# Sorting a step earlier in two equal parts, with the row transfers of a mixture-of-experts stage spaced by heads and tiles

## What is computed

```
# att1: 16 heads, q from x, k and v from the context
h = relu(out @ W1 + b1)
x = x + (h @ W2 + b2)
# moe1
xf = layernorm(x)                              # 2048 tokens of 128
routing = softmax(xf @ router_w.T)             # 8 experts
top_w, top_i = top_k(routing, 2); top_w /= sum(top_w)
h = silu(xf @ w_gate[e].T) * (xf @ w_up[e].T)  # 256 wide
x = x + sum over the two chosen e of top_w[e] * (h @ w_down[e].T)
```

## Time and profile before

| | us |
|---|---|
| median of 3 runs | 875.87 |
| lowest, highest | 874.03, 876.32 |
| profiled execution, its own time | 878.39 |
| its span, first to last instruction | 876.5 |

### The profile page before, as it was taken

How to read it: one execution, slowest core, us unless ns; L and a number is a source line. 1 busy time by engine, 2 the same in 40 slices (tenths; PEclk the granted TensorE clock), 3 DMA queues, 4 the chain that set the end, 5 groups by cost and what they waited for, 6 DMA issues and landing times. The chain is left out here.

```text
span 876.5 us, 14671 instructions
## 1 busy us (share of the span) xinstructions
PE 720.8 (82%) x4784; PEld 488.2 (56%) x4784; DVE 483.1 (55%) x1392; ACT 394.7 (45%) x837; POOL 238.3 (27%) x382
## 2 busy tenths in 40 slices
PE   1587888899988667978958787799999786779998
PEld 1355666566655435645525454567777675546665
DVE  4468676777777503623656874673335334444443
ACT  2465555466665525533424465353334554222221
POOL 4345454344321261224456643100001002000000
PEclk9999999999999977998967999799999999579999
DMA  9533224222230011222273320000000200023332
GB/s 294 140 96 86 64 65 117 70 69 68 76 85 16 11 46 46 88 82 82 70 193 87 90 75 2 1 1 1 1 0 1 82 0 1 1 79 104 97 94 63
DMA packets 76319, 57.94 MB, mean 66 GB/s; under 512 B 7400, under 2 KB 70120, under 8 KB 75768
## 3 DMA queue, kind: packets, MB, share of 16 engines
q1 hardware_dynamic: 74200, 52.85, 21.3%
q0 software_dynamic: 2048, 4.20, 1.5%
HBM read 25.37 MB, written 9.24 MB: 39 GB/s over the span
## 5 line engine op out<-in xcount | busy, mean ns | idle before, releaser
L909 DVE TENSOR_REDUCE negmax<-ps 128x2 f32<-128x512 f32 x256 | 169.8, 686 | 105.7 <-PE ps L1950 104.0
L1645 ACT ACTIVATE exps<-ps 128x512 f32<-128x512 f32 x256 | 148.3, 598 | 103.0 <-PE ps L1962 92.1
L1950 PE MATMUL ps<-stack 96*128 96x256 bf16 x512 | 102.6, 294 | 33.3 <-DVE negmax L909 19.3
L1962 PE MATMUL ps<-stack 99*128 99x256 bf16 x512 | 100.1, 286 | 22.6 <-DMA stack<-maxt 13.2
L1950 PEld LDWEIGHTS ps<-stack 96*128 96x128 bf16 x512 | 47.8, 103 | 58.2 <-DVE negmax L909 34.1
L1962 PEld LDWEIGHTS ps<-stack 99*128 99x128 bf16 x512 | 43.9, 101 | 63.8 <-DMA stack<-maxt 22.4
L1978 PE MATMUL ps<-exps,values 128*32 128x256 f32 x1024 | 72.9, 402 | 0.7 <-ACT exps L1645 0.7
L2203 PEld LDWEIGHTS ps<-pack_moe,ht 128*128 128x128 f32 x512 | 61.9, 191 | 15.8 <-issue 14.0
L1286 DVE SCALAR_TENSOR_TENSOR x_sb<-ps,weights,x_sb 128x128 f32<-128x128 f32 (+1 forms) x128 | 36.0, 344 | 61.7 <-PE ps L2203 61.6
L1819 ACT ACTIVATE ht<-ps,pack_moe 128x512 f32<-128x512 f32 x64 | 43.3, 686 | 57.5 <-PE ps L2291 56.0
L2203 PE MATMUL ps<-pack_moe,ht 128*128 128x128 f32 x512 | 62.3, 275 | 0.5 <-ACT ht L1819 0.5
(11 more groups left out here) (221 smaller groups left out, 1330.4 us busy)
## 6 DMA issues: line engine op xcount, KB each, us to landing
stack<-qk_parts SPq DMA_DIRECT2D x168, 128.0 KB
stack<-weights_t SPq DMA_DIRECT2D x32, 256.0 KB, 3.3
pack_moe<-in_moe SPq DMA_DIRECT2D x1, 3076.0 KB, 14.9
outputs_moe<-y_kept SPq DMA_DIRECT2D x46, 64.0 KB
ht<-gathered SPq DMA_DIRECT2D x22, 128.0 KB
gathered<-y_kept SPq DMA_DIRECT2D x10, 256.0 KB, 2.9
pack_moe<-in_moe SPq DMA_DIRECT2D x1, 2129.0 KB
pack_moe<-in_moe SPq DMA_DIRECT2D x1, 1732.0 KB, 6.9
```

The costliest lines, as they stand in the source:

```text
L909: dve.tensor_reduce(negmax_of[b % 2][:, :, h:h + 1].rearrange("p t h -> p (t h)"), ps[:, h % 2, :].rearrange("p (t k) -> p t k", t=2), AX, ...
L1645: nc.scalar.activation(exps[:, i, :], ps[:, 2 + h % 2, :], ACT.Exp, scale=scale)\
L1950: last = pe.matmul(ps[:, h % 2, t * T:(t + 1) * T], st[0:MAXROW, h, 0, t * P:(t + 1) * P], st[0:MAXROW, h, 1, :], start=True, stop=True)
L1962: last = pe.matmul(ps[:, 2 + h % 2, t * T:(t + 1) * T], st[0:MAXROW + 3, h, 1, t * P:(t + 1) * P], st[0:MAXROW + 3, h, 0, :], start=True, ...
```

## The change

The parts become equal: FIRST_PART = 4, 8 and 8 token tiles, 23 and 23 sorted tiles. Since the first part now needs only batches 0 to 3, its sorting stands a step earlier (the logits at (-1, 15), the two picks, the marks, the ranks and the places in step 0, the weights at (1, 12)), and the batches 4 to 6 are normalized at the end of the flow, with two more chunks turned in step 2. Of the tile loop's own sorting only the last two token tiles are normalized and turned there, and its steps come up to two tiles earlier.

The row transfers of the first part, now 16, are issued one every second beat from (0, 14), each with a wait on `cols_psum`, PE's count of the heads that have passed L1962. In the second part, also 16 now, and in the first 16 fetches, only every fourth waits for a tile (from tile 5 and from tile 25).

The offsets are read with three registers at (2, 6), and then with one load of one register behind the up product of each tile. Two waits are added in `turn_max` on PE, since a PSUM bank is shared otherwise.

The core of the diff:

```
@@ -80,11 +80,10 @@
...
 EXPERT = {"moe1": 768}
 PARTS = 2
-FIRST_PART = 5
+FIRST_PART = 4
 PART = (range(0, 2 * FIRST_PART), range(2 * FIRST_PART, NT))
-NORMED = (range(0, 8), range(8, 10), range(10, NT))
-CHUNKS = ((0, 1, 2, 3), (4, 5, 6, 7), (8, 9), (10, 11, 12, 13), (14, 15))
-FIRST_CHUNK = 3
+NORMED = (range(0, 8), range(8, 14), range(14, NT))
+CHUNKS = ((0, 1, 2, 3), (4, 5, 6, 7), (8, 9, 10, 11), (12, 13), (14, 15))
...
@@ -100,21 +99,23 @@
...
-SORT_STEPS = {"stats": ((-1, 6), (0, 3)), "rstd": ((-1, 7), (0, 4)), "norm": ((-1, 9), (0, 7)), "logits": (0, 12),
-              "top": (1, 1), "exp": (1, 1), "first": (1, 2), "second": (1, 3), "mark": (1, 3), "rank": (1, 7),
-              "place": (1, 4), "weigh": (1, 5), "load": (2, 6)}
-TURN_STEPS = ((-1, 11), (-1, 13), (0, 10))
-SEND_STEPS = ((1, 4, range(0, 5)), (2, 4, range(5, 10)))
+SORT_STEPS = {"stats": ((-1, 3), (2, 3)), "rstd": ((-1, 4), (2, 4)), "norm": ((-1, 8), (2, 6)), "logits": (-1, 15),
+              "top": (0, 1), "exp": (0, 2), "first": (0, 4), "second": (0, 6), "mark": (0, 8), "rank": (0, 9),
+              "place": (0, 11), "weigh": (1, 12), "load": (2, 6)}
+TURN_STEPS = ((-1, 10), (-1, 12), (2, 13), (2, 15))
+TURNED_STEPS = ((-1, 11), (-1, 13), (3, 0), (3, 1))
+SEND_FROM = 14
 ZERO_STEPS = range(-14, -2)
 ZEROINGS = len(ZERO_STEPS) + 1
-SORT_BEATS = {"norm": (-1, 0), "turn": (0, 1), "logits": 2, "top": 3, "exp": 3, "first": (4, 5), "second": (6, 7),
-              "mark": 7, "rank": 7, "place": (8, 9, 11), "weigh": 10}
-EARLY_TILES = (34, 35, 37, 38, 40, 41, 43, 45)
-JOIN_TILES = (32, 33, 35, 36, 38, 40, 42, 43)
+SORT_BEATS = {"turn": -1, "logits": 0, "top": 1, "exp": 1, "first": (2, 3), "second": (4, 4), "mark": 5, "rank": 5,
+              "place": (6, 7, 9), "weigh": 8}
+EARLY_TILES = (33, 34, 36, 37, 39, 41, 43, 45)
+JOIN_TILES = (30, 31, 33, 34, 35, 37, 39, 40)
 FETCHED_EARLY = 4
 IN_FLIGHT = 3
-SEND_TILE = 13
-FETCH_TILE = 27
+REGISTERS = 3
+SEND_TILE = 5
+FETCH_TILE = 25
...
@@ -523,7 +524,7 @@
...
             if s in SORTED:
-                return (TURN, TURN, TURN, 5, 6)[i]
+                return (TURN, TURN, 0, 1, 5)[i]
             return (0, 1, 0, 6)[i] if s in MOE else (6, SIDE, 6, 6)[i]
...
@@ -1198,14 +1200,12 @@
...
                 at = SORT_BEATS
-                if j in at["norm"]:
-                    apply_all(s, len(NORMED) - 1, CHUNKS[FIRST_CHUNK + at["norm"].index(j)])
                 if j == at["top"]:
                     route_logits(s, 1)
                 if j in at["first"]:
                     route_pick(s, 1, (0,), at["first"].index(j))
-                if j in at["second"]:
-                    route_pick(s, 1, (1,), at["second"].index(j))
+                if j == at["second"][0]:
+                    route_pick(s, 1, (1,))
                 if j == at["mark"]:
                     mark_picks(s, 1)
...
@@ -1469,9 +1470,9 @@
...
                             if (tail, u) == SORT_STEPS["rstd"][i]:
                                 make_rstd_all(nxt, i, NORMED[i])
-                        for at_tail, at_beat, tiles in SEND_STEPS if nxt in SORTED else ():
-                            if (tail, u) == (at_tail, at_beat):
-                                send_rows(nxt, 0, tiles)
+                        n, odd = divmod(16 * tail + u - SEND_FROM, 2)
+                        if nxt in SORTED and not odd and 0 <= n < 2 * len(GROUPS[nxt][0]):
+                            send_row(nxt, 0, n // 2, n % 2)
                         b = total + tail + 3
                         if flow == EARLY[0] and u in (3, 7) and valid(b) and b >= FETCHED_EARLY:
...
@@ -1496,20 +1497,22 @@
...
                         pool.tensor_tensor(kact, krelu, krelu, ALU.mult).then_inc(sem["kact_ready"], 1)
...
-            def send_rows(s, g, tiles):
-
-                if tiles[0] == GROUPS[s][g][0]:
+            def send_row(s, g, t, k):
+
+                n = 2 * (t - GROUPS[s][g][0]) + k
+                i, landed = sending(s, t, k)
+                if n == 0:
                     pool.wait_ge(zeros_out, 16 * ZEROINGS) if s == SORTED[0] and g == 0 else None
                     wait(pool, "placed_ready", s, 0, g)
-                for t in tiles:
-                    for k in range(2):
-                        i, landed = sending(s, t, k)
-                        if landed > 16:
-                            pool.wait_ge(sent[i], landed - 16)
-                        if g == 1:
-                            wait(pool, "taken_psum", s, 0, SEND_TILE + 2 * (t - tiles[0]) + k)
-                        at = bass.IndirectOffsetOnAxis(ap=placed[:, k, t:t + 1], axis=0)
-                        pool.indirect_dma_start(gathered[g], at, z[:, t, :], None).then_inc(sent[i], 16)
+                if landed > 16:
+                    pool.wait_ge(sent[i], landed - 16)
+                if g and n % 4 == 0:
+                    wait(pool, "taken_psum", s, 0, SEND_TILE + n)
+                else:
+                    done_heads = SEND_FROM + 2 * n - COL_BEAT[16]
+                    wait(pool, "cols_psum", "att" + s[3:], B - 2 + done_heads // 16, done_heads % 16)
+                at = bass.IndirectOffsetOnAxis(ap=placed[:, k, t:t + 1], axis=0)
+                pool.indirect_dma_start(gathered[g], at, z[:, t, :], None).then_inc(sent[i], 16)
...
             def fetch_output(s, t, k):
...
@@ -1524,7 +1527,7 @@
...
                     m, arrived = fetched(s, at // 2, at % 2)
                     pool.wait_ge(back_in[m], arrived)
-                if t < 2 * FETCHED_EARLY:
+                if t < 2 * FETCHED_EARLY and t % 2 == 0 and k == 0:
                     wait(pool, "taken_psum", s, 0, min(FETCH_TILE + 2 * t + k, ALL_TILES - 1))
                 at = bass.IndirectOffsetOnAxis(ap=placed[:, k, t:t + 1], axis=0)
...
@@ -1533,7 +1536,9 @@
...
                 make_rstd_all(s, len(NORMED) - 1, NORMED[-1])
-                send_rows(s, 1, GROUPS[s][1])
+                for t in GROUPS[s][1]:
+                    for k in range(2):
+                        send_row(s, 1, t, k)
                 for t in range(2 * FETCHED_EARLY):
                     for k in range(2):
...
@@ -1984,6 +1989,8 @@
...
             def turn_max(s, m):
                 wait(pe, "max_ready", s, m)
+                wait(pe, "placed_ready", "moe1", 0, 0) if (s, m) == ("att1", B - 1) else None
+                wait(pe, "route_exp_in", "moe1", 0, 0) if (s, m) == ("att1", B - 2) else None
                 rows_of = 3 * H[s]
                 for t in range(2):
...
@@ -2231,10 +2240,11 @@
...
             weights_at = {}
...
-            def load_experts(s, g):
-
-                tiles = slice(PART_AT[g], PART_AT[g] + TILES[g])
-                pe.wait_ge(sem["experts_ready"], done("experts_ready", s, 0, g))
+            def load_experts(s, tiles):
+
+                g = part_of(tiles.start)
+                if tiles.start == PART_AT[g]:
+                    pe.wait_ge(sem["experts_ready"], done("experts_ready", s, 0, g))
                 found = nc.values_load_multi_w_load_instructions(
                     expert_at[0:1, tiles], [mybir.EngineType.PE], min_val=0, max_val=(E - 1) * EXPERT[s],
...
@@ -2251,13 +2261,13 @@
...
                         pe.transpose(ps[:, 2, 0:P], taken[:, i, :], ident).then_inc(sem["taken_psum"], 1)
                     if 0 <= j + 1 < ALL_TILES:
-                        if j + 1 == PART_AT[1]:
-                            load_experts(s, 1)
                         pe.wait_ge(sem["taken_ready"], done("taken_ready", s, 0, j + 1))
                         pe.wait_ge(sem["h_ready"], done("h_ready", s, 0, j - 1)) if j >= 1 else None
...
                         pe.matmul(ps[:, (j + 1) % 2, :], taken_t[:, (j + 1) % 2, :], par(s, "experts")[:, bass.ds(at, 2 * T)],
                                   start=True, stop=True).then_inc(sem["up_psum"], 1)
+                        if j + 1 + REGISTERS < ALL_TILES:
+                            load_experts(s, slice(j + 1 + REGISTERS, j + 2 + REGISTERS))
                     if 0 <= j < ALL_TILES:
                         pe.wait_ge(sem["h_ready"], done("h_ready", s, 0, j))
...
```

More of the change, by code:

```diff
@@ L1615, in beat @@
                 if nxt in SORTED:
-                    if (tail, u) in TURN_STEPS:
-                        copy_all(nxt, [TURN_STEPS.index((tail, u))])
+                    if (tail, u) in TURNED_STEPS:
+                        copy_all(nxt, [TURNED_STEPS.index((tail, u))])
                     if sort_at("exp", tail, u):
@@ L1874, in turn_all @@
                         wait(pe, "zt_ready", s, 0, 0)
-                    if s in SORTED and 0 < i < FIRST_CHUNK:
-                        wait(pe, "zt_ready", s, 0, i - 1)
+                    if s in SORTED and i == 1:
+                        wait(pe, "zt_ready", s, 0, 0)
                     for k, t in enumerate(chunks_of(s)[i]):
@@ L2039, in beat @@
                         wait(pe, "zt_ready", sn, n)
```

(9 more changed lines are left out.)

15 lines of the change are left out of this document (8 added, 7 removed).

## The result

Over 20 runs of each, side by side, the changed kernel takes 874.88 us (870.41 to 878.04) and the kernel before 878.76 us (873.66 to 885.26): the ratio is 0.9951, 95% interval 0.9931 to 0.9970, some 4 us gained. I had forecast 865.8 us, which is ten gained on the 875.87 us that I had; the kernel before is itself 2.9 us slower in this comparison. The sign of the forecast was right in the first comparison and its size was not.

The account below looks back on a forecast made before the run. PE, busy 82% of the span, was taken as the bound, so its idle time could be won. Terms -5.5, -8.4, -1.1, +3.9 and +1.0 summed to -10.1, from 875.87 to 865.8 us; range 856 to 885.

Parts of the forecast that it names:

- The start of the tile loop: First sorted tile, after att1: its rows were to arrive at 328.3 instead of 333.77 us, -5.5, bounds -1 and -10.
- step 0's +4: Step 0, 273 to 291 us: earlier sorting makes DVE the bound and lengthens it by 4 us, bounds +2 and +6.
- The unnamed stall of 4.0 us: ACT's 3.99 us idle at 314.31, beside ten transfers in a row; spreading them was to save 4.0, bounds none and 5.3.
- the 5.8: Up to batch 6's residual, behind step 0: savings of 1.8 us from moved sorting and 4.0 from the ACT stall.
- The register load: Tiles 26 to 31: without the load of 19 registers and its aftermath, 16.6 us becomes the steady 8.2, -8.4.
- The rival with a large fixed part: PE's queue behind every up product: one-register loads cost too much to hide; 888 us at 1.3 us each, chance 0.14.
- The sixteen transfers beside tiles: Second part's transfers, all in one row from about tile 9.5: 0.24 us each, +3.9, bounds 0 and 7.0.
- My second rival: Rows of sixteen transfers and fetches cost more than rows of ten: 0.9 us each from the third, 883 us, chance 0.11.
- The waits by fours hold nothing back: Second part's sends: the waits for tiles 13 and 17 are already met, so all sixteen transfers go in one row.
- The rule on the two sides of SBUF: DMA and compute can't slow each other, so the -4.0 and +3.9 both fall away; the sum is then -10.0.
- the upper bound: Slow end of the forecast: tail at -1, transfers at +7 and +2.2, given as +0.7, some 876 us.
- the forecast's narrow range: Whole kernel: forecast with its bounds had chance 0.68, of which the middle, 860 to 872 us, had 0.50.

Follow-up runs that it names:

- e16: Changed kernel with the first part's transfers in two rows of eight at (1, 4) and (2, 4), without the waits for heads; 881.34 us, ratio 1.0037 to before.
- e1: Kernel before with only the offset loads changed: three registers at (2, 6), then one behind each up product; 861.45 us against 872.06, ratio 0.9888.
- e12: Same program as e1, run on a chip that stalls; 871.67 us, ratio 0.9913 to the kernel before.
- e6: Kernel before, unchanged, run for its trace on a second chip, which stalls; 879.7 us.
- e9: Kernel before, unchanged, run for its trace on a third chip, which stalls; 881.54 us.
- e15: Kernel before with offsets loaded tile by tile and its first sixteen fetches spaced by two small POOL operations each; 867.93 us, ratio 0.9876.
- e11: Changed kernel with one small POOL operation behind each second-part transfer and each of the first sixteen fetches, on a chip that stalls; 872.78 us, ratio 0.9924.
- e3: Changed kernel with six small POOL operations behind every fourth second-part transfer and every fourth of the first sixteen fetches; 863.11 us, ratio 0.9893.
- e8: Changed kernel, rerun on a third chip, which stalls; 875.38 us, ratio 0.9996 to the kernel before.
- e5: Changed kernel, rerun on a second chip, which stalls; 877.68 us, ratio 0.9994 to the kernel before.
- e13: Changed kernel, rerun on another chip that stalls; 876.21 us against 878.00 for the kernel before, ratio 0.9990.
- e7: Changed kernel with offsets in two bulk loads of 23 registers, on a third chip, which stalls; 880.27 us, ratio 1.0076 to the kernel before.
- e14: Changed kernel with two small POOL operations behind each transfer beside tiles and each of the first fetches; 866.02 us, ratio 0.9859 to the kernel before.
- e2: Changed kernel with offsets in two bulk loads of 23 registers, on the chip without stalls; 860.03 us, ratio 0.9881 to the kernel before.

## Why the prediction was right and wrong

**The start of the tile loop** was right in its mechanism and short in its size: -8.8 us instead of -5.5, counted from the first maxima of batch 6. The last transfer decided it, as worked out, which e16 bears out, and the five late ones behind the roots are there. The term that was too large is step 0's +4: DVE had room, and it cost +2.1 in these two traces. Even that is uncertain. From the first to the last maxima of batch 7 the old order took 18.5 us in three traces (before, e1, e12) and 20.1 in three others (e6, e9, e15), the new order 20.0 to 20.5 in ten of twelve (18.9 in e11, 21.6 in e3). The unnamed stall of 4.0 us is there on a chip that stalls (e12) and not on the one that doesn't (e1), in one and the same program. That it was the length of the row of ten is likely and not shown: e16's rows of eight brought none. The 1.5 us by which the gain up to batch 6's residual exceeds the 5.8 differs from one execution to the next: from the last maxima of batch 7 to that residual the changed kernel took 17.5 us here and in e8, 19.1 in e5 and e13.

**The register load** was right: -8.4 forecast, -7.5 in the trace (of which a first row of fetches, now earlier, takes a part), and 0.8 to 1.1% in e1, e12 and e7 against e8. The rival with a large fixed part had no ground: 0.31 us for one register. The Trainium skill, "DMA: Bandwidth & Descriptors", section "Latency and other measured facts", has a floor of some 600 ns for such a load. That is about twice the 0.31 us of this trace; by either the load hides.

**The sixteen transfers beside tiles** are the step that failed. I priced them at 0.24 us each, "as the nearer in length", for +3.9; the trace shows +12.9. The cost is not one of a transfer but of time spent in a row at 1.27 us: the row of twelve cost 1.0 us a transfer, the row of four behind it 0.3, and at 1.53 us apart sixteen cost next to nothing (e14). Beside tiles it sets in 3.2 us into the row and then takes 2.3 to 2.5 us of every 2.84. A price read beside att1, where PE was waiting for other things as well, didn't carry over to a stretch in which PE is the bound. My second rival had the size, at 12.6 us for this term, with a chance of 0.11. It too priced by the transfer, so that its number is near by luck in part. The row that should have weighed more was that of the fetches, which lie beside the same tiles, though its 0.44 us each gives no more than 7.0. The time it gave, 883, was too high in its other term: the fetches didn't go in one row of sixteen. The wait for tile 33 held (it was met at 403.14), as the fourth wait of the sends (for tile 17) did at 368.93, because the stalls had slowed the tiles. "The waits by fours hold nothing back" was wrong for that reason. The places, too, were ready at tile 11 and not 9.5 (the first transfer went out at 346.25, tile 11 had started at 345.99), which moved the row without changing it.

**The rule on the two sides of SBUF** (the Trainium skill, "SBUF — State Buffer", "SBUF: two separate sides") I had set against the reading that transfers slow PE. Here the measurement decides: on one chip, with two small operations between the transfers as the only difference, 1.27 against 1.53 us of spacing, 29.5 against 17.3 us for ten tiles. The rule itself speaks of SBUF's ports, and no run here shows that they were shared: what fell is my conclusion from it, that a stall can't be the transfers'. By what path a row of them holds back what waits for PE's results stays open.

**Sums that were wrong in the working.** By its own terms the upper bound is -1.0 - 8.4 - 1.1 + 7.0 + 2.2 = -1.3 (some 874.6), not +0.7. The low clock's 5.4 us between 322 and 334 do not come out of the row given: 6.15 less 3.4 is 2.7. And 12.35 us for 42 operations are 0.29 us each, not 0.26. None of the three would have saved the forecast.

**What was left out:** +3.4 us in att2, where no instruction moved. The stretch took 65.1 us after and 61.6 before. In e5, e8 and e13 it took 63.7, 63.8 and 61.0 us, in e6 and e9 62.0 and 62.1, so much of it is what one execution differs from another; the cause of the rest is open.

**The chance** put on the forecast's narrow range was too high for one more reason that I couldn't have read from one trace: chips differ here by more than the change does. One program had the ratio 0.9881 on one (e2) and 1.0076 on another (e7). The changed kernel itself was not run on the chip without stalls, where the forecast might have come true or been passed.

## What to carry to other kernels

Price a row of transfers by the row of the profile that stands beside the same kind of work, and by how long it goes on, not by an average over transfers. If an engine that is the bound runs beside POOL's indexed transfers, space these out, and look at when the last one must have landed: e14 won 1.3% over the changed kernel with two small operations behind each transfer and each of the first fetches, though it then waited 6.7 us for rows. Look also at what else stands in POOL's queue behind them, as e15 shows. Take the parts of a change one at a time: the single register loads alone gained 0.9 to 1.1% (e12, e1), more than the whole. And repeat a result of this size on another chip. A load of many registers ahead of one product is better cut into single loads behind the products.

## What the runs showed of the hardware

While indexed transfers of 128 rows went out 1.27 us apart beside tiles, ACT and DVE, which wait there for PE's results, stood idle for 2.3 to 2.5 us of every 2.84 in the first trace, and ten tiles took 28.5 to 30.7 us instead of 16.9 in six traces (that one, and five on three of the four chips). In each the first idle time began 3.2 us behind the start of the first transfer. On the fourth chip sixteen in a row passed beside tiles at 1.64 us each (e2). At 1.38 us apart most of the stall stayed (27.8 us), at 1.53 it was gone (17.3 us); beside fetches some was left at 1.48 and 1.49. A load of one register took 0.31 us in the median of the trace after (0.30 at the least); one of 23 took 5.55 us in one place and 2.35 us in another of the same kernel (e7), so its length isn't set by the count alone. A small POOL operation of 0.2 us behind a transfer added some 0.11 us to the period (e11, 1.38 for 1.27).
